# Attention scores from plain fp32 matmuls on one copy of queries and keys, in place of three fp32r matmuls on high and low parts

## What is computed

```python
xn  = layernorm(x, g_in)
q   = (xn @ Wq) as 16 heads of 64        # 128 x 1024
k,v = split(xn @ Wkv)                    # 128 x 64 each, with a null key and a null value ahead
sim = q @ k.T + bias                     # 16 heads x 128 x 129, causal and padding masks
out = softmax(sim) @ v                   # 16 heads x 128 x 64
L(x)= layernorm(out @ Wo, g_out)
```

## Time and profile before

| | before |
|---|---|
| median of 3 runs | 2741.52 us (2741.1 to 2742.61) |
| the profiled execution: time, span | 2742.6 us, 2740.8 us |
| mean granted TensorE clock | 0.986 of full speed |
| busy PE, PE weight loads | 2631.8 us (96%), 2232.8 us (81%) |
| busy DVE, ACT, POOL | 2261.4 us (83%), 1822.9 us (67%), 1306.8 us (48%) |
| PE instructions | 15521 matmuls and as many weight loads |

### The profile page before, as it was taken

One profiled execution on the slowest core, in us unless ns is written; L12 is line 12 of the kernel. 1 busy time (PEld: TensorE's weight loads), 2 busy tenths in 40 slices (PEclk: granted clock), 3 DMA queues, 4 the chain that ended last, 5 costly groups with the idle time before them and its releaser, 6 DMA issues.

```text
span 2740.8 us, 50424 instructions
## 1 busy us (share of the span) xinstructions
PE 2631.8 (96%) x15521; PEld 2232.8 (81%) x15521; DVE 2261.4 (83%) x4918; ACT 1822.9 (67%) x6621; POOL 1306.8 (48%) x1174
## 2 busy tenths in 40 slices
PE   2699999999999999999999999999999999999997
PEld 1588888888888888888888888888888888888885
DVE  7588888888888888888888888888888888888885
ACT  2466766766766766766676676676676676676664
POOL 5344544544544544544444444454454454454452
PEclk7899999999999999999999999999999999999998
DMA  6000000000000100000101001000001001000000
GB/s 207 25 23 28 22 30 28 28 24 28 29 23 28 32 20 28 32 20 28 31 20 31 28 20 32 28 20 32 28 20 32 28 20 32 28 26 26 28 24 12
DMA packets 67237, 83.59 MB, mean 30 GB/s; under 512 B 26352, under 2 KB 29456, under 8 KB 67216
## 3 DMA queue, kind: packets, MB, share of 16 engines
q1 hardware_dynamic: 63264, 80.96, 9.5%
q10 hardware_dynamic: 3952, 2.38, 0.3%
HBM read 49.74 MB, written 16.79 MB: 24 GB/s over the span
## 4 chain that ended last, share of the span: by engine, by line
PE 95%; ACT 1%; issue 1%; DVE 1%; DVEq 0%
PE psum L297 30%; PE psum L358 26%; PE psum L327 14%; PE psum L346 9%; PE psum L337 8%; PE psum L311 4%; PE psum L285 2%; ACT probs L434 1%; PE psum L305 0%; DVE probs L557 0%; DVE neg_max L563 0%; ACT probs L441 0%; DVE x L596 0%; DVE bn_in L468 0%; DVE x_lo L480 0%
## 5 line engine op out<-in xcount | busy, mean ns | idle before, releaser
L636 POOL TENSOR_TENSOR probs<-probs,den_inv 128x512 f32<-128x512 f32 x512 | 516.8, 1041 | 1366.3 <-DVE den_inv L568 1366.2
L434 ACT ACTIVATE probs<-probs,neg_max 128x129 f32<-128x129 f32 x2048 | 797.4, 391 | 110.3 <-DVE neg_max L563 101.8
L629 POOL TENSOR_TENSOR masked_bias<-bias,pad_neg 128x512 f32<-128x512 f32 x512 | 690.2, 1378 | 15.3 <-POOL pad_neg L624 9.2
L434 ACT ACTIVATION_READ_ACCUMULATOR probs<-probs,neg_max 128x1 f32 x2048 | 382.8, 187 | 0.0
L557 DVE TENSOR_TENSOR probs<-psum,masked_bias 128x512 f32<-128x512 f32 x512 | 340.6, 686 | 50.9 <-PE psum L327 44.9
L297 PE MATMUL psum<-w_hi,x_hi 128*128 128x384 f32 (+1 forms) x1536 | 343.2, 345 | 3.9 <-DVE x_lo L480 3.9
L563 DVE TENSOR_REDUCE neg_max<-probs 128x4 f32<-128x516 f32 x512 | 343.0, 681 | 0.0
L297 PE MATMUL psum<-w_lo,x_hi 128*128 128x384 f32 (+1 forms) x1536 | 336.7, 341 | 0.0
L297 PE MATMUL psum<-w_hi,x_lo 128*128 128x384 f32 (+1 forms) x1536 | 336.7, 341 | 0.0
L393 ACT CAST x_hi<-psum 128x512 fp32r<-128x512 f32 x128 | 75.1, 587 | 349.4 <-PE psum L285 349.3
L327 PE MATMUL psum<-k_hi,q_hi 128*128 128x256 f32 x1024 | 293.9, 287 | 8.0 <-DVE k_lo L536 2.0
(11 more groups left out here) (116 smaller groups left out, 4543.2 us busy)
## 6 DMA issues: line engine op xcount, KB each, us to landing
xa<-in_x_dram SPq DMA_DIRECT2D x64, 256.0 KB, 2.8
x_res<-in_x_dram SPq DMA_DIRECT2D x64, 256.0 KB, 2.6
x_res<-x SPq DMA_DIRECT2D x64, 256.0 KB, 2.3
out_dram<-x_out SPq DMA_DIRECT2D x64, 256.0 KB, 2.0
raw<-in_L_cond_Wq_dram SPq DMA_DIRECT2D x8, 512.0 KB, 7.9
raw<-in_L_cond_Wo_dram SPq DMA_DIRECT2D x8, 256.0 KB, 2.9
raw<-in_L_cond_Wout_dram SPq DMA_DIRECT2D x8, 256.0 KB, 5.6
bias<-in_L_cond_w_dram SPq DMA_DIRECT2D x1, 1024.0 KB, 12.1
```

What stands on the lines that cost most here:

```text
L434: e = nc.scalar.activation(probs[:, h, :], probs[:, h, :], ACT.Exp, bias=neg_max[:, h:h + 1], accum_out=den[:, h:h + 1])
L629: m = nc.gpsimd.tensor_tensor(masked_bias[:, heads, :], bias[u.layer][:, heads, :], pad_neg[:, :].unsqueeze(1).to_broadcast([P, CH, S]), A ...
L636: nc.gpsimd.tensor_tensor(probs[:, c * CH:(c + 1) * CH, 0:S], probs[:, c * CH:(c + 1) * CH, 0:S], den_inv[:, c * CH:(c + 1) * CH].unsqueez ...
```

## The change

The scores become one plain fp32 matmul for each pair of heads, instead of three fp32r matmuls. `keys` takes the place of `k_hi` and `k_lo`, `q_t` that of `q_hi` and `q_lo`. ACT's copy of the queries stays, now into plain fp32; DVE's `split_kt` and `split_qt` are gone, and `scores`, `project` and `transpose_x` wait for the copies alone. A memset of the setup goes too. Lines of the changed kernel have other numbers.

```diff
             def scores(u, chunks):
-                wait(pe, k_lo_done, u.done)
+                wait(pe, keys_ready, u.done)
                 for c in chunks:
-                    wait(pe, q_lo_done[c // 2], u.done)
+                    wait(pe, qt_copied[c // 2], u.done)
...
                     for jj in range(2):
                         j = 2 * c + jj
-                        for n, (qs, ks) in enumerate(((q_hi, k_hi), (q_lo, k_hi), (q_hi, k_lo))):
-                            m = nc.tensor.matmul(SP[c % 2][:, jj * 2 * S:(jj + 1) * 2 * S], qs[:, j * P:(j + 1) * P], ks[:, :],
-                                                 start=(n == 0), stop=(n == 2))
+                        m = nc.tensor.matmul(SP[c % 2][:, jj * 2 * S:(jj + 1) * 2 * S], q_t[:, j * P:(j + 1) * P], keys[:, :],
+                                             start=True, stop=True)
                     m.then_inc(scores_done[c], 1)
...
                     wait(act, qt_done[g], u.done)
-                    nc.scalar.copy(q_hi[:, g * 512:(g + 1) * 512], Q[g][:, :]).then_inc(q_hi_done[g], 1)
+                    nc.scalar.copy(q_t[:, g * 512:(g + 1) * 512], Q[g][:, :]).then_inc(qt_copied[g], 1)
...
-                    t = nc.vector.tensor_scalar(k_hi[e * DH:(e + 1) * DH, e * S:(e + 1) * S], Q[2][e * DH:(e + 1) * DH, 0:S],
+                    t = nc.vector.tensor_scalar(keys[e * DH:(e + 1) * DH, e * S:(e + 1) * S], Q[2][e * DH:(e + 1) * DH, 0:S],
                                                 k_scale[u.layer][e * DH:(e + 1) * DH, 0:1], None, ALU.mult)
-                t.then_inc(k_hi_done, 1)
-
-            def split_kt(u):
-                wait(dve, k_hi_done, u.done)
...
-            def split_qt(u):
-                for g in range(2):
-                    wait(dve, q_hi_done[g], u.done)
...
+                t.then_inc(keys_ready, 1)
```

More of the change, by code:

```diff
@@ L159, in build @@
         root_col = sb("root_col", [P, 1])
-        k_hi = sb("k_hi", [P, 2 * S], F32R)
-        k_lo = sb("k_lo", [P, 2 * S], F32R)
+        keys = sb("keys", [P, 2 * S])
         xa = sb("xa", [P, D])
@@ L172, in build @@
             bias=bias, g_out=g_out, null_bias=null_bias, k_scale=k_scale, null_v=null_v, null_v_col=null_v_col, ident=ident,
-            eps_col=eps_col, root_col=root_col, k_hi=k_hi, k_lo=k_lo, psum=psum))
+            eps_col=eps_col, root_col=root_col, keys=keys, psum=psum))
         x_res = sb("x_res", [P, D])
@@ L183, in build @@
         q_sb = sb("q_sb", [P, INNER])
-        q_hi = sb("q_hi", [P, INNER], F32R)
-        q_lo = sb("q_lo", [P, INNER], F32R)
+        q_t = sb("q_t", [P, INNER])
         k_dup = sb("k_dup", [P, 2, DH])
@@ L220, in build @@
         k_ready, s0_scaled, s0_done = sem("k_ready"), sem("s0_scaled"), sem("s0_done")
-        kt_done, k_hi_done, k_lo_done = sem("kt_done"), sem("k_hi_done"), sem("k_lo_done")
+        kt_done, keys_ready = sem("kt_done"), sem("keys_ready")
         qt_done = [sem(f"qt_done{n}") for n in range(2)]
-        q_hi_done = [sem(f"q_hi_done{n}") for n in range(2)]
-        q_lo_done = [sem(f"q_lo_done{n}") for n in range(2)]
+        qt_copied = [sem(f"qt_copied{n}") for n in range(2)]
         pad_neg_done, masked_bias_done = sem("pad_neg_done"), sem("masked_bias_done")
@@ L282, in transpose_x @@
                 wait(pe, xn_done, u.done)
-                wait(pe, k_lo_done, u.prev)
+                wait(pe, keys_ready, u.prev)
                 for c in range(KC):
@@ L291, in project @@
                     if b < 2:
-                        wait(pe, q_lo_done[b], u.prev)
+                        wait(pe, qt_copied[b], u.prev)
                     lo, hi = QB[b]
@@ L528, in take_kt @@
                 for e in range(2):
-                    t = nc.vector.tensor_scalar(k_hi[e * DH:(e + 1) * DH, e * S:(e + 1) * S], Q[2][e * DH:(e + 1) * DH, 0:S],
+                    t = nc.vector.tensor_scalar(keys[e * DH:(e + 1) * DH, e * S:(e + 1) * S], Q[2][e * DH:(e + 1) * DH, 0:S],
                                                 k_scale[u.layer][e * DH:(e + 1) * DH, 0:1], None, ALU.mult)
-                t.then_inc(k_hi_done, 1)
-            def split_kt(u):
-                wait(dve, k_hi_done, u.done)
[L535 to L540, removed]
-            def split_qt(u):
-                for g in range(2):
-                    wait(dve, q_hi_done[g], u.done)
-                    nc.vector.tensor_tensor(q_lo[:, g * 512:(g + 1) * 512], Q[g][:, :], q_hi[:, g * 512:(g + 1) * 512].bitcast(F32),
-                                            ALU.subtract).then_inc(q_lo_done[g], 1)
+                t.then_inc(keys_ready, 1)
             def place_s0(u):
@@ L604, in body @@
                            (part(inverse_sum, 3), b_old), (take_kv, a), (end_finish, a_prev), (input_statistics, b_new),
-                           (normalise, b_new), (take_kt, a), (split_kt, a), (split_qt, a),
+                           (normalise, b_new), (take_kt, a),
                            (part(split_o, (0,)), b_old), (place_s0, a), (part(add_bias, 0), a), (part(add_bias, 1), a),
@@ L612, in body @@
                            (unit_q(2), b_new), (norms(0), b_new), (unit_q(0), b_new), (norms(1), b_new),
-                           (take_kt, b_new), (unit_q(1), b_new), (part(split_o, (0,)), a), (split_kt, b_new),
-                           (part(split_o, (1,)), a), (split_qt, b_new), (unit_s0, b_new))
+                           (take_kt, b_new), (unit_q(1), b_new), (part(split_o, (0,)), a),
+                           (part(split_o, (1,)), a), (unit_s0, b_new))
             run_units(dve, body, NB)
@@ L651, in setup @@
         v[n] for n in ("w_hi", "w_lo", "wo_hi", "wo_lo", "bias", "g_out", "null_bias", "k_scale"))
-    null_v, null_v_col, ident, eps_col, root_col, k_hi, k_lo, psum = (
-        v[n] for n in ("null_v", "null_v_col", "ident", "eps_col", "root_col", "k_hi", "k_lo", "psum"))
+    null_v, null_v_col, ident, eps_col, root_col, keys, psum = (
+        v[n] for n in ("null_v", "null_v_col", "ident", "eps_col", "root_col", "keys", "psum"))
     layers = (L0, L1)
@@ L825, in _ @@
                           last_layer, diagonals_transposed]
-                step(V.memset(k_hi[:, :].bitcast(F32), 0.0))
-                step(V.memset(k_lo[:, :].bitcast(F32), 0.0))
+                step(V.memset(keys[:, :], 0.0))
                 step(V.memset(eps_col[:, :], EPS))
```

## The result

| | before | after |
|---|---|---|
| median of 4 runs | 2742.07 us | 2793.0 us (2792.06 to 2795.09) |
| the profiled execution: time, span | 2742.6, 2740.8 us | 2792.06, 2790.3 us |
| granted clock | 0.986 | 0.987 |
| one turn of the loop | 40.84 us | 41.68 us |
| DVE busy | 2261.4 us | 2041.4 us |

The changed kernel is slower by a ratio of 1.0186, with an interval of 1.0168 to 1.0204; that is 51 us. A turn (one unit a and one unit b) is read off the starts of the scores of a: 1305.91 to 1346.75 us before, 1327.15 to 1368.83 after. The means over 61 turns are 40.83 and 41.68 us.

The account below looks back on a forecast made before the run. PE's stream of matmuls bounds the kernel; 2742.6 + 78 - 13 - 9 - 2 = 2796.6 us, so a median of 2796 us. Its own range was 2782 to 2818 (chance 0.65), for 8 in 10 2768 to 2838.

Parts of the forecast that it names:

- The bound: PE's stream of matmuls, busy for 96% of the span; a change to it should reach the time almost whole.
- The price of a pair: Scores on PE: two plain instructions, 0.433 us, replace three fp32r matmuls, 0.357 us; 1024 pairs, +78 us.
- The wait for q_lo: PE's wait ahead of unit a's scores: 0.20 us recovered (ends 0.10 and 0.32), 63 times, -13 us.
- what leaving the 64-column matmuls costs anyway: Between values and scores of a: a deduction from the recovered wait, which no row shows without a wait.
- The waits around the values of a: Values' second half and transposes of q: 0.14 us of 0 to 0.20 recovered, 64 times, -9 us.
- the projection caps the gain at 0.20 us: ACT's read of b's first projection restarts the chain; only 0.20 us of backlog can absorb a later PE.
- The end pieces: First unit, where the q and k splits stand bare (1.4 us), and last unit: together -2 us.
- Costs at the seams: Rival, chance 0.15: 0.1 us per entry into a scores block, +26 us, or stretched passes; 2822 to 2842 us.
- The sign of failing: Scores' rows over 0.23 or under 0.2 us apart, or new waits behind the longer scores.
- More comes back: Rival, chance 0.11: all named waits vanish, gaining 56 us instead of 22; time 2762 us.
- Two passes instead of four: Rival, chance 0.04: plain matmul streams two times, a pair costs 0.245 us; 2603 us.
- bare weight loads: Rival, chance 0.02: each scores instruction pays its unhidden load, 2 x 0.19 us a pair, +389 us; 3185 us.

Follow-up runs that it names:

- The run with one matmul for a pair: Kernel before with one fp32r matmul per pair of heads (high by high) and no low parts: 2629.49 us, ratio 0.9592.
- the cross of runs: Changed kernel with DVE's q and k splits put back, 2793.6 us; kernel before without low parts, three matmuls kept, 2738.81 us.
- late waits: Kernel before, matmuls reordered high-high, high-low, low-high, each wait moved to the first matmul needing its tile: 2733.82 us, ratio 0.9964.

## Why the prediction held, and where it did not

**The bound.** PE's stream, right in the direction of this change. The run with one matmul for a pair shows how one-sided that was: the text said "a change to what PE streams should reach the time almost whole", and of 244 us taken away only 113 arrived. That sentence needed a sign. "Almost whole" was too strong in the growing direction too: of 77 us of matmuls 51 arrived, and the text's own sum had 54 of 78.

**The price of a pair.** Forecast 0.433 us against 0.357, +78 us. The b block shows 0.43 and 0.355, and the mean of all blocks, +1.20 us in 16 pairs, is 0.075 us a pair, 77 us in all. An instruction of the plain matmul takes 0.215 to 0.216 us at 256 columns. At 2.4 GHz 0.2156 us are 517 cycles, twice the columns and five more, so the fixed part is near nothing. The two rows that carried this, the setup's matmuls and the values, were other shapes at 512 columns, and scaled. The rule of the Trainium skill on the gap (TensorE: Matmul & The Clock Gate, Back-to-back issue gap), taken for 512 passed columns, gives 0.2158 us for an instruction, and the trace agrees. The section calls it the gap of an isolated matmul and gives 131 ns at 512 columns for a stream; no stream here is that fast. Where the rule fails is on the fp32r matmuls, 0.119 us against its 0.109, and so a sum by the rule alone would have been 34 us too high.

**The wait for q_lo.** Forecast 0.20 us a turn, -13 us. Measured 0.13 from values to scores, and the first block of scores kept 0.03 us of its own, so 0.10 us and about -6 us, the lower end of the term. The step that was mis-sized is "less what leaving the 64-column matmuls costs anyway": in the new timeline the last instruction of the values starts 0.62 us before their listed end, at 1326.60, its columns have passed at 1327.03, and the scores start only at 1327.15, with their second instruction also late (the block takes 1.84 us, not the 1.72 of a b block). The lower end of 0.10 us, not the 0.20 taken, had the price of that exit in it. The 0.08 us at the second matmul were part of the exit too: they stay where no matmul waits. The runs with late waits and without `q_lo` show the same 1.88 to 1.89 us from values to scores, so this is what the passage costs when nothing is waited for.

**The waits around the values of a.** Forecast 0.14 us of 0 to 0.20, -9 us; measured 0.11 in the turn shown and 0.10 in the mean, -7 us. That it hangs on PE's longer scores the cross of runs shows: with DVE's work put back the 0.11 us stay, and with DVE relieved but PE not later they don't appear. But the working was wrong, and that the number came out is luck. The text had the chain of ACT and DVE start with the first chunk of the scores of a, PE later by some 0.4 us and the chain not at all. In the traces both come later, counted from the first score of a. The values of a start 17.33 us behind it before and 17.93 after. ACT's last copy, which their second half needs, ends at 18.44 us and 18.92. So PE is 0.60 us later and the chain 0.48. The chain starts anew with the third chunk: its masked bias is added on DVE 0.04 us behind the chunk's last matmul, in every turn of both kernels (two lines of before, then two of after).

```profile
1309.37 0.28 PE L327 MATMUL psum<-k_lo,q_hi 128*128 128x256 f32 x1
1309.69 0.69 DVE L557 TENSOR_TENSOR probs<-psum,masked_bias 128x512 f32<-128x512 f32 x1
...
1331.41 0.69 DVE L538 TENSOR_TENSOR probs<-psum,masked_bias 128x512 f32<-128x512 f32 x1 [0.28 <-PE psum L323]
1345.01 1.06 ACT L437 COPY probs<-psum 128x512 f32<-128x512 f32 x2
```

That addition starts 3.78 us behind the first score before and 4.26 after, and the same 0.48 us runs through the exponentials to the copy. So the chain takes on the growth of three chunks of the scores of a, and only that of the fourth, two pairs or 0.15 us, less small pieces, comes back. Of the two waits themselves, put at 0.30 and 0.26 us, the run with `end_finish` moved shows 0.49 together. That the projection caps the gain at 0.20 us, as the text said, no run tests.

What the text did not see was a third place of the same kind. The second transposes of b's probabilities, and the transposes of q ahead of them, came closer by 0.10 us a turn, some 6 us, again with DVE's work put back and not where PE is no later. The two errors nearly cancel: 0.20 + 0.14 = 0.34 us a turn were forecast, and 0.13 - 0.03 + 0.11 + 0.10 = 0.31 came. That the total fits so closely is luck.

**The end pieces.** -2 us forecast, -4 to -5 measured. With DVE's work put back the ends are only 0.9 us longer again, and the runs of one kernel differ by 3 us among themselves, so what shortened the ends is open.

**The rivals.** Costs at the seams: the plain matmuls enter and leave the fp32r stream without any (a block with the group behind it grows by 0.29 to 0.30 us, and four pairs at 0.075 are 0.30); the first block of a, behind the 64-column values, grows by 0.33. The sign of failing, new waits behind the longer scores, showed on DVE, whose waits for the scores ahead of adding the bias grew from 45 to 77 us in all, but not on PE. More comes back: it can be had, but not by this change; it takes another instruction's move. Two passes instead of four, and bare weight loads: a step of 0.215 us excludes both, the first by a factor of nearly two.

## What to carry to other kernels

Price a matmul by the distance between starts in a dense stretch and by columns times passes; here three fp32r passes cost 0.357 us and one plain fp32 matmul, which passes its columns four times, 0.431. An engine at 96% says nothing on what stands behind it: before counting on a shorter stream, look for the chains that end just before it needs them. And when a slower engine gives time back, ask first whether it merely comes later to the same wait; here one instruction's place on DVE was worth more than half of what the whole change cost.

## What was unexpected in the hardware

The DVE instruction of `end_finish` took 1820 ns in its old place, beside POOL's mask additions, and 743 ns in the new one, where POOL is idle. In the old place it began at 1319.33 us, while the second of POOL's additions was starting. In the last turn POOL has nothing left to add, and there the same instruction, in the same place of the list, takes 0.75 us at 2705.57. These are DVE's and POOL's lines of the kernel before:

```profile
1319.33 1.85 DVE L596 SCALAR_TENSOR_TENSOR x_out<-x_out,rstd_out,x_res 128x512 f32<-128x512 f32 x1
1319.35 1.28 POOL L629 TENSOR_TENSOR masked_bias<-bias,pad_neg 128x512 f32<-128x512 f32 x1
1320.59 1.74 POOL L629 TENSOR_TENSOR masked_bias<-bias,pad_neg 128x512 f32<-128x512 f32 x1
...
2705.57 0.75 DVE L596 SCALAR_TENSOR_TENSOR x_out<-x_out,rstd_out,x_res 128x512 f32<-128x512 f32 x1
```

So it is POOL beside it that costs the 1.1 us, and POOL pays as well: the addition behind it takes 1.73 us in the mean, and 1.30 with `end_finish` moved. The Trainium skill names the cause (SBUF — State Buffer, Who interferes with whom, and SBUF: two separate sides): a DVE instruction with two inputs in SBUF and a GpSimd instruction that reads SBUF exclude each other for a whole instruction. The trace agrees with it in size: waiting for the addition at 1319.35 to end, and then 0.74 us of its own, would make some 2.0 us, an estimate from these lines, against 1.85.

fp32r matmuls are not at the rate of the clock (0.119 us for 256 columns, 0.107 by 2.4 GHz), while plain fp32 ones are within about 1% (0.2156 us for 512 passed columns, 0.213 by 2.4 GHz), at the same granted clock. No run here says why.

Matmuls on row halves of the array run side by side in plain fp32: 16 instructions of 64 rows and 128 columns in 1.10 us, with entry and exit, against 1.72 for the 8 that they replace. In the middle of such a block they start in pairs 0.112 us apart, which is 0.224 us for a pair of heads and what that run's theory had. Behind the last of them the next group starts only after 0.20 us, and its second instruction is late as well.
